# A sparse-attention block: the subtraction of the row maximum is issued on GpSimd instead of VectorE

## The reference, cut to what matters

```python
xn = layernorm(x)                                  # 32 x 256 x 128
q, k, v = heads(xn @ Wqkv.T + bqkv)                # 16 heads of 8
q, k = layernorm(q, q_gamma, q_beta), layernorm(k, k_gamma, k_beta)
aw  = softmax(q @ k.T / sqrt(8))                   # 256 x 256 for each head
kth = top_k(aw, 12)[..., -1:]                      # the 12th largest of each row
aws = aw * (aw >= kth); aws = aws / (aws.sum(-1) + 1e-8)
o_s = aws @ v                                      # the sparse branch
o_l = (softmax(q) @ (softmax(k).T @ v)) / (z + 1e-6)   # the linear branch
a   = sigmoid(alpha)
y   = x + (a * o_s + (1 - a) * o_l) @ Wproj.T + bproj + (xn @ W[idx] + b[idx])
```

## Time and profile before

| what | us |
|---|---|
| median of 3 runs (1332.71 to 1335.28) | 1333.5 |
| profiled execution: from its first to its last instruction | 1331.1 |
| DVE busy | 1260.1 (95%) |
| ACT busy | 1138.5 (86%) |
| GpSimd busy | 1110.9 (83%) |
| PE busy | 1040.0 (78%) |

### The profile page before, as it was taken

The page is one execution under the profiler, slowest core; times in us unless marked ns, Lnnn a source line. Parts: engine busy times, 40 slices in busy tenths (PEclk is TensorE's granted clock), DMA queues, the critical chain, the costliest instruction groups (busy, mean ns, idle before and its releaser), DMA issues.

```text
span 1331.1 us, 40027 instructions
## 1 busy us (share of the span) xinstructions
PE 1040.0 (78%) x8964; PEld 693.5 (52%) x8964; DVE 1260.1 (95%) x4916; ACT 1138.5 (86%) x3978; POOL 1110.9 (83%) x1458
## 2 busy tenths in 40 slices
PE   3787877778787878877888787777877788787776
PEld 1455555555455555555555455554555555555544
DVE  5799999999999999999999999999999999999995
ACT  3689998989899888989989899888989888898885
POOL 4588898979789888888879889798888888889874
PEclk9989999989899798998989989898998998989998
DMA  2222222112222122221112221112221212221210
GB/s 57 72 59 63 77 77 75 35 57 64 77 76 72 29 64 65 76 77 47 53 53 76 77 76 46 55 57 71 76 76 35 66 53 76 77 76 33 64 49 13
DMA packets 165131, 82.31 MB, mean 62 GB/s; under 512 B 7747, under 2 KB 164933, under 8 KB 164934
## 3 DMA queue, kind: packets, MB, share of 16 engines
q1 hardware_dynamic: 164934, 80.54, 20.9%
HBM read 42.77 MB, written 37.75 MB: 60 GB/s over the span
## 4 chain that ended last, share of the span: by engine, by line
DVE 57%; issue 33%; DVEq 6%; ACT 1%; POOL 1%; PE 1%; DMA 0%; SPq 0%; POOLq 0%
DVE rest L525 21%; DVE top L518 21%; DVE next L531 8%; DVEq L72 5%; DVE drop L615 2%; DVE o_sparse L574 1%; ACT e L719 1%; DVE den L566 1%; DVE k_sum L593 1%; DVE stats L582 0%; PE work_ps L910 0%; PE work_ps L911 0%; DVE x_mv L588 0%; DVE d_max L557 0%; DVE den L571 0%
## 5 line engine op out<-in xcount | busy, mean ns | idle before, releaser
L386 POOL TENSOR_SCALAR below<-e,next 128x256 bf16<-128x256 f32 x768 | 696.1, 922 | 21.5 <-DVE next L531 21.3
L719 ACT ACTIVATE e<-score_ps,drop 128x256 f32<-128x256 f32 x1024 | 472.4, 480 | 108.2 <-DVE drop L615 105.5
L838 PE MATMUL turn_ps<-ident,e 128*128 128x128 f32 x2048 | 429.9, 303 | 10.9 <-ACT kept L685 10.4
L525 DVE MATCH_REPLACE8 rest<-e 128x256 f32<-128x256 f32 x1024 | 413.3, 404 | 0.0
L531 DVE MAX8 next<-rest 128x8 f32<-128x256 f32 x1024 | 407.5, 408 | 0.0
L839 PE MATMUL turn_ps<-minus_huge,below 128*128 128x128 bf16 x2048 | 402.5, 232 | 0.0
L518 DVE MAX8 top<-score_ps 128x8 f32<-128x256 f32 x1024 | 359.4, 410 | 41.8 <-issue 21.7
L838 PEld LDWEIGHTS turn_ps<-ident,e 128*128 128x128 f32 x2048 | 312.2, 152 | 80.9 <-ACT kept L685 17.9
L685 ACT ACTIVATE kept<-turn_ps 128x512 f32<-128x512 f32 x512 | 285.1, 620 | 33.8 <-PE turn_ps L839 14.3
L839 PEld LDWEIGHTS turn_ps<-minus_huge,below 128*128 128x128 bf16 x2048 | 234.5, 115 | 0.0
L719 ACT ACTIVATION_READ_ACCUMULATOR e<-score_ps,drop 128x1 f32 x1024 | 217.1, 212 | 0.0
(11 more groups left out here) (141 smaller groups left out, 1540.6 us busy)
## 6 DMA issues: line engine op xcount, KB each, us to landing
part_slots<-part SPq DMA_DIRECT2D x128, 192.0 KB, 2.3
q_slots<-part_slots SPq DMA_DIRECT2D x64, 256.0 KB, 3.4
k_slots<-part_slots SPq DMA_DIRECT2D x64, 256.0 KB, 4.1
part_slots<-part SPq DMA_DIRECT2D x64, 128.0 KB, 1.9
x_sb<-in_L_attn_x SPq DMA_DIRECT2D x32, 128.0 KB, 3.6
x_res<-in_L_attn_x SPq DMA_DIRECT2D x32, 128.0 KB, 3.7
out_y<-out_sb SPq DMA_DIRECT2D x32, 128.0 KB, 4.2
w_ops<-in_L_ffn_W SPq DMA_DIRECT2D x1, 512.0 KB
```

What stands on the lines that cost most here:

```text
L386: nc.gpsimd.tensor_scalar(below[:, r, t, :], e[:, r, t, :], next8[:, r, t, TOPK - 9:TOPK - 8], None, ALU.is_lt).then_inc(s["below_pool"], 1)
L525: nc.vector.match_replace(rest[:, t, :], e8[:, (u_ - 1) % 2, t, :], e[:, (u_ - 1) % RING, t, :], REMOVED).then_inc(s["rest_ready"], 1)
L719: nc.scalar.activation(e[:, u_ % RING, t, :], score_ps[:, u_ % 2, t // 2, t % 2, :], ACT.Exp, bias=drop[:, u_ % 2, t, 0:1], accum_out=z[:, ...
L838: mm(dst, e[:, r, t, keys], ident[:], start=True, stop=False, is_transpose=True)
```

## The change

The subtraction leaves DVE's queue and becomes the first instruction of each of GpSimd's slots. GpSimd waits there for the four MAX8 of the slot (`top_ready`) and for ACT to have read the buffer of two slots ago (`e8_ready`). DVE gets a wait for `drop_ready` of two slots ago ahead of its MAX8 (the buffer `top` is used again then). GpSimd waits once at the start for its own constants, since it now reads `top`.

```diff
@@ GpSimd, set-up
             nc.gpsimd.memset(eps_row[:, :, D:VA], Z_EPS).then_inc(s["pool_const"], 1)
+            pool.wait_ge(s["pool_const"], 7)
@@ GpSimd, body
                 for u_ in range(UNITS):
                     g = it * UNITS + u_
+                    if exists(it):
+
+                        q = u_ % 2
+                        wait(pool, s["e8_ready"], g - 1)
+                        wait_alone(pool, s["top_ready"], TILES * (g + 1), s["waits_passed"])
+                        nc.gpsimd.tensor_tensor(drop[:, q], top[:, q], top[:, q, :, 1:2].to_broadcast(
+                            [P, TILES, 9]), ALU.subtract).then_inc(s["drop_ready"], 1)
                     if u_ == 0 and exists(it + 1):
@@ VectorE, body
                     if exists(it):
+                        wait(dve, s["drop_ready"], g - 1)
                         for t in range(TILES):
                             largest(g, q, t)
                     if before:
                         remove(u_, 0)
-                    if exists(it):
-
-                        dve.wait_ge(s["top_ready"], TILES * (g + 1))
-                        nc.vector.tensor_tensor(drop[:, q], top[:, q], top[:, q, :, 1:2].to_broadcast(
-                            [P, TILES, 9]), ALU.subtract).then_inc(s["drop_ready"], 1)
                     extra(u_, 0)
```

## The result

The changed kernel takes 1364.9 us (median of 4 runs, 1359.5 to 1367.8), against 1333.1 for the kernel before (4 runs beside it, 1331.4 to 1335.3). The ratio is 1.0248, with a 95% interval of 1.0219 to 1.0277. So it is slower by 32 us. I had forecast 1318, with a range of 1296 to 1346; the forecast missed by 47 us, in the wrong direction.

A forecast was written before the change was run, and what follows sets the result against it. DVE, busy 95% of the span, sets the pace, with GpSimd and ACT close behind. The mean pair of batches loses 1.0 us; 15.5 pairs take 15.5 us from 1331.1, giving 1315.6, median 1318 us; range 1296 to 1346.

The forecast's parts named there:

- the subtraction on GpSimd: Each 36-element `drop` on GpSimd takes 265 ns, between bounds of 194 and 324 ns.
- the slower rival: Each `drop` costs GpSimd's queue 194 ns more, through port or waits; kernel 1349 us; chance 23%.
- the chain of GpSimd's first five slots: GpSimd's steps from slot 0's MAX8 to the end of slot 4's `drop`, summed to 20.5 us.
- T: The end of slot 0's four MAX8 on DVE, from which the prediction measures all times in a batch.
- DVE's two new waits: DVE waits 0.5 us at `d_max` for `qkn` and 0.4 us at slot 5's `den` for PE's transposes.
- e8: ACT's exponential of the eight largest scores; the prediction had no term for a wait of DVE for it.
- Behind this `e` hangs a chain that I leave as long as it was: From ACT's `e` of slot 4 to PE's scores of the next slot 0: 16.6 us, unchanged.
- ACT's waits for `drop` cost nothing but what is counted in the chain: ACT's waits for GpSimd's `drop` add no time beyond the 20.5 us chain up to slot 4.
- the wait ahead of the next slot 0: DVE arrives at T + 36.5 and waits for PE's scores, there at T + 37.2.
- the hole: DVE's idle gap at the loop's jump back, every second batch, 2.6 to 2.7 us.
- the last load is hidden from PE: The batch's last keys land at T + 36.3, before the scores start at T + 36.8; 0.5 us left.
- The gain that I had booked: DVE's queue gives up 61 us in all with its `drop`, 1.9 us for each batch.

The follow-up runs named there:

- Experiment 9: Changed kernel with only slot 5's subtraction moved ahead of the small steps at the end of slot 4: 1344.7 us, ratio 1.0079 to the kernel before.
- experiment 16: Changed kernel with slot 5's subtraction moved ahead of slot 4's small steps and the loop written out: 1301.8 us, ratio 0.9736 to the kernel before.
- Experiment 4: Changed kernel with unused PE transposes, 14 ahead of its wait for `o_sum` and 8 ahead of `qkn`: 1354.3 us, ratio 1.0186 to the kernel before.
- experiment 11: Changed kernel with the loop written out and unused PE transposes ahead of its waits for `o_sum` and `qkn`: 1320.3 us, ratio 0.9921.
- Experiment 17: Changed kernel with the second half of the `q` and `k` slots loaded behind the batch's first MAX8, away from the jump: 1354.2 us, ratio 1.0175.
- experiment 3: Kernel before, with GpSimd waiting at each slot's head for DVE's MAX8, then making an unused subtraction; DVE keeps its own: 1338.7 us, ratio 1.0061.
- experiment 2: Kernel before, with only GpSimd's wait for DVE's MAX8 at each slot's head; the subtraction stays on DVE: 1355.1 us, ratio 1.0185.
- 5: Kernel before with all batches written out, so that no engine jumps back: 1308.8 us, ratio 0.9829.
- 6: Changed kernel with all batches written out, so that no engine jumps back: 1320.8 us, ratio 0.992 to the kernel before.
- experiment 18: Kernel before with the loads of the second half of the `q` and `k` slots held until DVE's jump: 1333.1 us, ratio 1.0017.
- experiment 7: Kernel before without any subtraction of the maximum; ACT takes the exponential of the score itself, overflow guard left out: 1268.8 us, ratio 0.9535.

## Why the prediction was wrong

**Right: the subtraction on GpSimd** (249 ns, forecast 265), and with it the slower rival's reason is refuted: neither the wait nor the port adds 0.1 us for each. The slower side was right, its mechanism not. **Right: the chain of GpSimd's first five slots**; the `drop` of slot 4 ends at T + 20.07 in the batch shown, forecast 20.5. **Right: `qkn`** at T + 16.7 and 16.1, forecast 16.5. Of DVE's two new waits, the one at `den` is there and larger: 29.7 us in all, against 7.4 before. (I had added it too small besides: `den` at T + 24.7 less six subtractions of 0.24 and plus 0.5 is T + 23.8, a wait of 0.7 us and not 0.4.) The one at `d_max`, 0.5 us in my sum, does not show in the trace, which has no idle time ahead of `d_max`. Instead DVE waits 17.6 us for ACT's `e8` (before: 0.9), which I did not have.

**Wrong: "Behind this `e` hangs a chain that I leave as long as it was", and "ACT's waits for `drop` cost nothing but what is counted in the chain".** I took the `drop` of slots 0 to 4 for the chain and stopped there. The next one, drop(5), stands behind `residue`, all of `below` and the small steps of slot 4, and ends at T + 26.5 and 26.7, where DVE had made it at 24.0 and 24.7. ACT's `e` of slot 5 waits for it, behind that come `v_aug`, PE's transposes of `xn` and the next batch's scores. The sum saw the wait ahead of the next slot 0, for scores that end at T + 37.2. They end at T + 37.7 and 38.4, but DVE idles only 0.1 us for them in even batches, and in odd ones they lie within the hole. It had lost the time before: in the odd batches most of all ahead of `den` in slot 7, behind PE's transposes of what ACT hands on late. Experiment 9 moved this one instruction (it ends 1.4 us earlier) and gave back 20 us; experiment 16 did so without jumps, 19 us.

**Wrong: the chain taken at the old speed of PE.** I had `qkn` three microseconds later and asked what that did to DVE's `d_max`, but not what PE does meanwhile. In odd batches it waits (2.93 us in the one shown, 2.7 in the mean), and behind the wait its granted clock is mostly the lower level: in the batch shown the turns take 0.42 us each, `kept` and `part` are late, and `e` of slot 4 starts 1.3 us after its `drop` is there (0.9 in the mean of the odd batches, 0.1 in the even ones, whose clock stayed at 1.00). In even batches the wait is the one for `o_sum`, and the low clock behind it makes the scores of slot 3 late: DVE's 1.1 us there are a wait that my sum did not have at all. Experiment 4, which fills PE's waits, gave back 11 us; in the unrolled kernel the same edit (experiment 11) gave back nothing. This is a cost that no busy time shows beforehand.

**Wrong: the term "the hole", kept at 2.6 us.** It became a stall of 3.76 us in place of 2.89, 12 times: 10.4 us. The later writes and loads of the slots now run beside the jump. I had asked whether the last load is hidden from PE, not what it lies beside. Experiment 17 gave back 11 us.

The three edits gave 20, 11 and 11 us when made one at a time in the changed kernel, against a miss of 47. They were not made together, so I can't say that they add up; the first two can hide each other, as experiment 4's even batches show. GpSimd's tie to DVE and its work are not the whole price: both together, with ACT served by DVE as before, cost 8 us (experiment 3), and most of the 24 us of the tie alone (experiment 2) are DVE's own subtraction held up. What the changed kernel has besides is that ACT takes each `drop` from the tied queue. That this is what takes DVE's gain and the rest of the 32 us follows by exclusion, and for drop(5) from experiment 9. Unrolled, the change still costs 12 us (5 and 6).

The gain that I had booked came only in part: DVE's busy time fell by 44 us, where I had 61. Its four large groups of 1024 instructions each are 3 or 4 ns longer in the mean (`rest` 407 in place of 404, `next` 412 and 408, `top` 414 and 410, the load ahead of `rest` 72 and 69), some 14 us in sum, which would be most of the other 17; why they are longer is open. All of it and more turned into idle time (75 us), at the places given above.

## What to carry to other kernels

When a step moves to another in-order queue, the price is not its 0.25 us, and here not the wait that ties the queue alone (8 us for both, while nobody needed what the step made: experiment 3). It is above all how late the consumer gets it: write down for every slot when the consumer gets it, to the last one, not up to the one that was late before. Ask of each engine that is made to wait what it does right behind the wait (PE's clock here), and of each transfer that is pushed back what it now lies beside. A wait at the head of a slot ties the whole queue; one step made some 1.4 us earlier was worth 20 us here, while moving six of the eight by a reading of the old trace cost 44. And an experiment that leaves the old step in place can change it: read what the tie did to DVE's own subtraction before calling the difference the tie's.

## What the runs showed of the hardware

- **A jump back in a loop costs DVE 2.9 us** from its branch to its next instruction, control included (12 jumps in the kernel before; the engine itself is idle for 2.7 us), and more in most cases with transfers beside it. Over 156 jumps of 13 kernels (all but those of experiments 17 and 18) the stall's mean was 2.9 us where the DMA engines were busy for under a fifth of the 2.5 us from the branch on, 3.6 us at 0.4 to 0.5 and 4.2 above; the correlation is 0.81. With experiments 17 and 18, 180 jumps, it is 0.64. Without jumps the kernel before takes 0.9829 of its time, 23 us less.

  The Trainium skill, Runtime: NRT & Kernel Launch, section Instruction fetch mechanics, offers a cause: a taken branch to a place outside the small window of instructions held makes the engine fetch them by a DMA before it goes on. Experiments 5 and 17 agree with it, if such a fetch shares the DMA engines with the loads; no run here shows the fetch itself, and experiment 18, with 3.18 us at a share of 0.75, shows that sharing alone does not fix its length.
- **A small subtraction on DVE was held up by some of GpSimd's instructions and not by others.** In the kernel before, of 256 `drop` (median 184 ns) 47 took 331 ns or more and ended with a TENSOR_TENSOR that GpSimd had begun earlier; of 149 that began beside a TENSOR_SCALAR of GpSimd (`below` mostly) the median was 181 ns and the longest 483.
- **Leaving out the per-row bias made ACT's exponential shorter**: 394 ns in experiment 7, in place of 480 in the kernel before and 491 in the changed one, for the same 128x256 elements from the same place. The group of experiment 7:

```profile
L718 ACT ACTIVATE e<-score_ps 128x256 f32<-128x256 f32 x1024 | 380.4, 394 | 128.9 <-DVE top L518 100.9
```

  That is 92 us of ACT's time, and a possible part of why experiment 7 won more than DVE's subtraction was worth; the two were not separated. The Trainium skill, ScalarE: Activation LUTs, section What ACT_TABLE_LOAD costs, gives about 93 ns for an operand per partition; the 86 to 97 ns here agree.
